# A two-layer conditioned linear attention kernel: transposes of the queries and of h by halves, a later film load, and a rearranged last unit

## The reference

```
xn = layernorm(x)
q = softmax over each head's channels (xn @ Wq + bq)
k = softmax over the tokens (xn @ Wk + bk, masked)
v = masked (xn @ Wv + bv)
att = per head: k^T v            (head size x head size)
y = per head: q att
scale, shift = split(silu(emb) @ W_emb + b_emb)      one row for each sequence
h = silu(layernorm(y) * (1 + scale) + shift)
x = x + h @ W_out + b_out
```

## Time and profile before

| | us |
|---|---|
| median of 3 runs | 811.47 (810.06 to 811.48) |
| the profiled execution | 811.12 |
| its span, first to last instruction | 809.2 |
| TensorE (PE) busy in it | 766.0 |
| VectorE (DVE) busy | 698.7 |
| ScalarE (ACT) busy | 517.0 |
| GpSimd (POOL) busy | 438.4 |

### The profile page before, as it was taken

How to read it: one execution, slowest core, us unless ns; L and a number is a source line. 1 busy time by engine, 2 the same in 40 slices (tenths; PEclk the granted TensorE clock), 3 DMA queues, 4 the chain that set the end, 5 groups by cost and what they waited for, 6 DMA issues and landing times.

```text
span 809.2 us, 16851 instructions
## 1 busy us (share of the span) xinstructions
PE 766.0 (95%) x6359; PEld 371.6 (46%) x6359; DVE 698.7 (86%) x1421; ACT 517.0 (64%) x1011; POOL 438.4 (54%) x432
## 2 busy tenths in 40 slices
PE   4997979999999999998999999999999999999986
PEld 2445434354444445444454544444454544444442
DVE  6898967798998999999988898888888899888985
ACT  4897763856748687686866685565657476560723
POOL 2475573553856658487563755447265535544352
PEclk9997989999999999999999999999999999999999
DMA  9966497664967759596594939588584939485542
GB/s 320 307 130 187 116 257 220 131 147 135 183 171 139 165 153 183 170 180 173 111 187 119 195 106 175 167 153 200 96 192 117 183 119 182 117 150 139 89 120 79
DMA packets 291201, 130.73 MB, mean 162 GB/s; under 512 B 261392, under 2 KB 261776, under 8 KB 291120
## 3 DMA queue, kind: packets, MB, share of 16 engines
q1 hardware_dynamic: 288384, 125.27, 68.7%
q10 hardware_dynamic: 2736, 4.39, 1.6%
HBM read 47.74 MB, written 16.88 MB: 80 GB/s over the span
## 4 chain that ended last, share of the span: by engine, by line
PE 80%; DVE 10%; issue 3%; ACT 3%; DMA 2%; POOL 1%; SPq 0%; DVEq 0%; ACTq 0%; POOLq 0%
PE ring L529 72%; PE ring L699 3%; PE att_ps L648 2%; DMA sb_ht_parts<-sb_htok 2%; DVE sb_k_or_qt L1021 1%; ACT sb_k_or_qt L1410 1%; DVE sb_q_sum L1080 1%; DVE sb_row_peak L868 1%; DMA sb_x<-in_x 1%; DVE sb_ht_parts L1134 1%; PE att_ps L590 0%; PE film_ps L590 0%; DVE sb_q_max L1054 0%; DVE ring L1051 0%; PE film_ps L599 0%
## 5 line engine op out<-in xcount | busy, mean ns | idle before, releaser
L529 PE MATMUL ring<-sb_w_hi,sb_xt_parts 128*128 128x512 f16 x1024 | 309.0, 379 | 0.0
L529 PE MATMUL ring<-sb_w_lo,sb_xt_parts 128*128 128x512 f16 x512 | 194.0, 379 | 0.0
L529 PE MATMUL ring<-sb_w_hi,sb_ht_parts 128*128 128x512 f16 x512 | 158.3, 384 | 10.0 <-DMA sb_ht_parts<-sb_htok 5.8
L529 PEld LDWEIGHTS ring<-sb_w_hi,sb_xt_parts 128*128 128x128 f16 x1024 | 100.3, 98 | 126.1 <-issue 6.6
L529 PE MATMUL ring<-sb_xt_parts,sb_w_hi 128*128 128x512 f16 x496 | 149.9, 384 | 8.6 <-issue 8.1
L1662 POOL TENSOR_TENSOR sb_htok<-sb_ht_parts,sb_htok 128x512 f16<-128x512 f32 x60 | 75.2, 1275 | 137.7 <-ACT sb_htok L1443 137.7
L1678 POOL TENSOR_TENSOR sb_tanh<-sb_v_or_q,sb_kq_hi 128x512 f16<-128x512 f32 x64 | 74.0, 1157 | 88.2 <-ACT sb_kq_hi L1474 87.6
L529 PE MATMUL ring<-sb_w_lo,sb_ht_parts 128*128 128x512 f16 x256 | 98.3, 384 | 0.0
L529 PE MATMUL ring<-sb_xt_parts,sb_w_lo 128*128 128x512 f16 x248 | 95.2, 384 | 0.0
L529 PEld LDWEIGHTS ring<-sb_w_hi,sb_ht_parts 128*128 128x128 f16 x512 | 50.7, 99 | 71.6 <-issue 9.7
L1467 ACT ACTIVATE sb_v_or_q<-ring,sb_ln_one 128x512 f32<-128x512 f32 x64 | 43.9, 686 | 61.6 <-DVE ring L1056 60.7
(11 more groups left out here) (230 smaller groups left out, 1403.1 us busy)
## 6 DMA issues: line engine op xcount, KB each, us to landing
out<-sb_x SPq DMA_DIRECT2D x14, 1024.0 KB, 4.8
sb_rows_now<-film_rows SPq DMA_DIRECT2D x16, 512.0 KB, 4.4
sb_x<-out SPq DMA_DIRECT2D x8, 1024.0 KB, 5.2
sb_x<-in_x SPq DMA_DIRECT2D x7, 1024.0 KB, 5.7
sb_mask_add<-mask_terms SPq DMA_DIRECT2D x15, 256.0 KB, 5.5
sb_w_stage<-in_L_cond_Wk SPq DMA_DIRECT2D x2, 1024.0 KB, 9.0
sb_w_hi<-in_L_cond_W_emb SPq DMA_DIRECT2D x1, 1536.0 KB, 13.1
sb_w_lo<-in_L_cond_W_emb SPq DMA_DIRECT2D x1, 1536.0 KB, 14.2
```

What stands on the lines that cost most here:

```text
L529: last = nc.tensor.matmul(out, lhs, rhs, start=(n == 0), stop=(n == len(pairs) - 1))
```

## The change

- `turn_q` and `turn_h` take a half j (0 or 1) and turn two token tiles, high and low. Each half has semaphores of its own. `ht_parts` is laid out by halves, so the first half of h overwrites y's tiles 0 and 1 only, and may be turned when these are split.
- TensorE waits for h by halves in `output` and for the queries by halves in `attend`.
- On SP, the film rows are loaded ahead of h (except in units 3 to 5), and the second half of x goes between the two halves of the queries.
- ScalarE asks for the second part of layer 1's film matrix behind the attention matrix of unit 1 instead of behind its values.
- Unit 14's output tiles use banks 0, 1, 0, 1. In unit 15, VectorE masks the attention matrix directly behind the queries' sums, and takes the reciprocals and residual 0 after it; GpSimd adds unit 15's output bias in unit 14; and `attended(LAST, 2)` comes ahead of the first low part of h.

```diff
-BANKS = {"K": (0, 1, 2, 3), ..., "Y": (2, 3, 4, 5), "last": (2, 3, 4, 5)}
+BANKS = {"K": (0, 1, 2, 3), ..., "Y": (2, 3, 4, 5), "next": (0, 1, 0, 1), "last": (2, 3, 4, 5)}
-    elif name == "O" and unit == LAST:
-        name = "last"
+    elif name == "O" and unit >= LAST - 1:
+        name = "last" if unit == LAST else "next"
...
-        ht_parts = sb("ht_parts", [P, 2, T, C, P], F16)
+        ht_parts = sb("ht_parts", [P, 2, 2, T // 2, C, P], F16)
...
-            def turn_h(u):
-                if u == 1:
+            def turn_h(u, j):
+                if j:
+                    pass
+                elif u == 1:
                     sp.wait_ge(v_lo_ready, 4)
                 else:
                     sp.wait_ge(done["O"], 4 * (u - 1))
-                sp.wait_ge(h_lo_ready, 4 * u)
-                turn(ht_hi.rearrange("p t c m -> p (t c) m"), flat_h[0], h_hi_ready, 4 * u, ht_hi_ready)
-                turn(ht_lo.rearrange("p t c m -> p (t c) m"), flat_h[1], h_lo_ready, 4 * u, ht_lo_ready)
+                h_count = 4 * (u - 1) + 2 * j + 2
+                sp.wait_ge(h_lo_ready, h_count)
+                for n, ready, turned in ((0, h_hi_ready, ht_hi_ready), (1, h_lo_ready, ht_lo_ready)):
+                    turn(ht_parts[:, j, n].rearrange("p t c m -> p (t c) m"), flat_h[n][:, 2 * j * D:2 * (j + 1) * D], ready, h_count, turned[j])
...
-            def turn_q(u):
-                sp.wait_ge(kt_hi_ready, 16 * (u + 1))
-                sp.wait_ge(kt_lo_ready, 16 * (u + 1))
-                turn(blocks_of(qt_hi), kq_hi[:], q_hi_ready, 4 * (u + 1), qt_hi_ready)
-                turn(blocks_of(qt_lo), q_lo, q_lo_ready, 4 * (u + 1), qt_lo_ready)
+            def turn_q(u, j):
+                if j == 0:
+                    sp.wait_ge(kt_hi_ready, 16 * (u + 1))
+                    sp.wait_ge(kt_lo_ready, 16 * (u + 1))
+                at = slice(2 * j * D, 2 * (j + 1) * D)
+                turn(blocks_of(qt_hi[:, at]), kq_hi[:, at], q_hi_ready, 4 * u + 2 * j + 2, qt_hi_ready[j])
+                turn(blocks_of(qt_lo[:, at]), q_lo[:, at], q_lo_ready, 4 * u + 2 * j + 2, qt_lo_ready[j])
...
                 turn_k(u)
-                turn_h(u)
+                if not PREP <= u < PREP + 3:
+                    sp.wait_ge(z_ready, 4 * u)
+                    load_rows(u)
+                turn_h(u, 0)
+                turn_h(u, 1)
...
-                sp.wait_ge(z_ready, 4 * u)
                 if PREP <= u < PREP + 3:
+                    sp.wait_ge(z_ready, 4 * u)
                     sp.wait_ge(shift_summed, 3 + u - PREP + 1)
-                load_rows(u)
+                    load_rows(u)
                 if u < LAST:
                     turn_x(u, 0)
-                turn_q(u)
+                turn_q(u, 0)
                 if u < LAST:
                     turn_x(u, 1)
+                turn_q(u, 1)
+                if u < LAST:
                     sp.wait_ge(x_new, 4 * u)
...
             def output(unit, tiles=range(T), between=lambda i: None):
-                project_tokens("O", unit, O_, ht_hi, ht_lo, tiles, between)
+                for t in tiles:
+                    if unit < LAST:
+                        pe.wait_ge(ht_hi_ready[t // 2], 16 * (unit + 1))
+                        pe.wait_ge(ht_lo_ready[t // 2], 16 * (unit + 1))
+                    project_tokens("O", unit, O_, ht_hi, ht_lo, (t,), between)
...
             def attend(u, between=lambda t: None):
-                pe.wait_ge(qt_hi_ready, 16 * (u + 1))
-                pe.wait_ge(qt_lo_ready, 16 * (u + 1))
...
                     if t % 2 == 0:
+                        pe.wait_ge(qt_hi_ready[t // 2], 16 * (u + 1))
+                        pe.wait_ge(qt_lo_ready[t // 2], 16 * (u + 1))
                         take_bank("Y", t, u)
...
                 query_sums(u)
+                mask_attention(u)
+                query_recip(u)
                 residual(u - 1, 0)
-                mask_attention(u)
                 residual(u - 1, 1)
...
-                last_h_low(0)
                 attended(LAST, 2)
+                last_h_low(0)
                 last_h_low(1)
...
                 high_values(u, range(T))
-                if u == 1:
-                    load_film_w(1, 1)
-                elif prepares is not None:
+                if prepares is not None:
                     copy_shift(1, prepares)
...
                 high_attention(u)
+                if u == 1:
+                    load_film_w(1, 1)
...
                 add_bias(u)
+                if u == LAST - 1:
+                    add_bias(LAST)
...
                 low_queries(u)
-                add_bias(u)
                 low_attention(u)
```

More of the change, by code:

```diff
@@ L70, in order @@
     return front + tiles_of("O", u - 1) + tiles_of("Y", u)
-BANKS = {"K": (0, 1, 2, 3), "first": (4, 5, 0, 1), "second": (2, 3, 4, 5), "O": (2, 3, 0, 1), "Y": (2, 3, 4, 5), "last": (2, 3, 4, 5)}
+BANKS = {"K": (0, 1, 2, 3), "first": (4, 5, 0, 1), "second": (2, 3, 4, 5), "O": (2, 3, 0, 1), "Y": (2, 3, 4, 5), "next": (0, 1, 0, 1), "last": (2, 3, 4, 5)}
 def bank_of(name, i, unit):
@@ L226, in build @@
         xt_hi, xt_lo = xt_parts[:, 0], xt_parts[:, 1]
-        ht_hi, ht_lo = ht_parts[:, 0], ht_parts[:, 1]
-        ht_f32 = ht_parts[:].rearrange("p n t c m -> p (n t c m)").bitcast(F32).rearrange("p (t d) -> p t d", t=T)
+        xt_tiles = [[xt_parts[:, n, t] for t in range(T)] for n in range(2)]
+        ht_hi, ht_lo = ([ht_parts[:, t // 2, n, t % 2] for t in range(T)] for n in range(2))
+        ht_f32 = ht_parts[:].rearrange("p j n t c m -> p (j n t c m)").bitcast(F32).rearrange("p (t d) -> p t d", t=T)
         tok_f32 = tok[:].rearrange("p n t d -> p (n t d)").bitcast(F32)
@@ L316, in build @@
         k_hi_ready, k_lo_ready, q_hi_ready, q_lo_ready = sem("k_hi_ready"), sem("k_lo_ready"), sem("q_hi_ready"), sem("q_lo_ready")
-        kt_hi_ready, kt_lo_ready, qt_hi_ready, qt_lo_ready = (
-            sem("kt_hi_ready"), sem("kt_lo_ready"), sem("qt_hi_ready"), sem("qt_lo_ready"))
+        kt_hi_ready, kt_lo_ready = sem("kt_hi_ready"), sem("kt_lo_ready")
+        qt_hi_ready, qt_lo_ready = ([sem(f"{name}{j}") for j in range(2)] for name in ("qt_hi_ready", "qt_lo_ready"))
+        ht_hi_ready, ht_lo_ready = ([sem(f"{name}{j}") for j in range(2)] for name in ("ht_hi_ready", "ht_lo_ready"))
         k_top_ready, k_shift_ready, k_exp, k_sum_scaled, k_recip_ready = (
@@ L767, in step @@
                     pe.wait_ge(w_ready[1], 2)
-                project_tokens("V", u, V_, xt_hi, xt_lo)
+                project_tokens("V", u, V_, *xt_tiles)
                 if u == B:
                     pe.wait_ge(w_ready[1], 3)
-                project_tokens("Q", u, Q_, xt_hi, xt_lo, between=with_q)
+                project_tokens("Q", u, Q_, *xt_tiles, between=with_q)
                 if shifted is not None:
@@ L1263, in tail @@
                 gate(LAST, 1)
+                attended(LAST, 2)
                 last_h_low(0)
-                attended(LAST, 2)
                 last_h_low(1)
@@ L1415, in high_keys @@
                 if u:
-                    act.wait_ge(qt_hi_ready, 16 * u)
+                    for j in range(2):
+                        act.wait_ge(qt_hi_ready[j], 16 * u)
                 for i in range(C):
@@ L1426, in tanh_of @@
                 elif unit == LAST:
-                    act.wait_ge(qt_lo_ready, 16 * UNITS)
+                    for j in range(2):
+                        act.wait_ge(qt_lo_ready[j], 16 * UNITS)
                 elif t == 0:
@@ L1439, in high_h @@
                 if t == 0 and unit:
-                    act.wait_ge(ht_hi_ready, 16 * unit)
+                    for j in range(2):
+                        act.wait_ge(ht_hi_ready[j], 16 * unit)
                 elif t == 0:
@@ L1656, in low_h @@
                 if unit:
-                    pool.wait_ge(ht_lo_ready, 16 * unit)
+                    for j in range(2):
+                        pool.wait_ge(ht_lo_ready[j], 16 * unit)
                 else:
```

27 lines of the change are left out of this document (14 added, 13 removed).

## The result

Before: 810.33 us, median of 20 runs (807.81 to 811.64). After: 815.33 us, median of 20 runs (811.20 to 819.75). The ratio is 1.0069 [1.0055, 1.0083]: the change made the kernel slower by 0.7%. Forecast were 798.0 and a range of 792 to 805. The runs after lie further apart than those before; the profiled execution, 813.17 with a span of 811.3, is one of the quicker ones, so it shows some 2 of the 5 us that the medians differ by.

The account below looks back on a forecast made before the run. TensorE, busy 95% of the span, was taken as the bound, so only its holes and halved clock could go. -9.5 - 2.0 - 1.5 = -13.0 us from 811.12 gave 798.1, stated as 798.0; range 792.0 to 805.0.

Parts of the forecast that it names:

- What bounds the kernel: TensorE, busy 95% of the span; 8.3 us of holes at unit starts await x's second half, last in SP's queue.
- Twelve halves at 1.4 are 16.8, so SP is through at 734.3: SP's queue, unit 14: started at 717.5, the last half lands at 736.2, before it is wanted at 737.95; holes close.
- the sum's largest term, -9.5: Unit starts: 8.3 us of holes and 1.7 of halved clock go, 0.5 given back for stray waits; bounds 0 to -10.0.
- rival (c): Middle of attend: last landing no earlier, +0.76 in ten units, 817.2 us, if a half costs over 1.55 us; chance 0.06.
- The load of the film rows moves into the pause of SP between the keys and h: SP's queue, each unit: 0.75 us of issue plus its transfer leaves the stretch between h and x, a gain.
- (a): Unit 1: the film matrix does no harm among the transposes, so the unit gives 7.7 us; 792.4 us, chance 0.14.
- (b): Only part of the holes closes: half of 9.5, nothing in unit 1, 1.0 at the end; 805.3 us, chance 0.14.
- (d): Nothing moves: holes lie inside TensorE's queue, not x's landing, and the tail's gain goes to the clock; 811 us, chance 0.04.
- Waits that are added: TensorE's waits per half of h in output and of q in attend; said of h's halves that they cost nothing.
- Unit 1: Wait for h goes, freeing 7.7 us, but the film matrix delays x's and q's transposes: -2.0 us, bounds +1 and -7.7.
- The last unit: Unit 15: earlier mask and freed banks start attend 2.2 us earlier, partly lost to clock: -1.5 us, bounds 0 and -2.3.

Follow-up runs that it names:

- a4_xfirst: Kernel before, whole transposes, with x's second half issued ahead of the queries: 814.92 us, ratio 1.0056.
- b2_xlast: a3_halves with both halves of the queries ahead of x's second half: 812.12 us, ratio 1.0020 to the kernel before.
- b3_rowsk: Kernel before with the film rows loaded ahead of the keys' transposes (except units 3 to 5): 810.00 us, ratio 0.9998.
- a3_halves: Changed kernel without its film-matrix and last-unit edits, so SP's order and the halves only: 818.70 us, ratio 1.0102 to the kernel before.
- b4_halves_rowsk: a3_halves with the film rows loaded ahead of the keys' transposes: 805.59 us, ratio 0.9943 to the kernel before.
- c1_after_rowsk: Changed kernel with only the film rows moved ahead of the keys' transposes: 802.10 us, ratio 0.9897 to the kernel before.
- d1_before_twice: Kernel before with a second, unread load of the film rows right behind the first in units 9 to 15: 813.46 us, ratio 1.0048.
- d2: Changed kernel with a second, unread load of the film rows right behind the first in units 9 to 15: 825.18 us, ratio 1.0212 to the kernel before.
- b1_rowsold: a3_halves with the film rows loaded behind h, as before the change: 813.04 us, ratio 1.0037 to the kernel before.
- a2_film: Kernel before with only the film matrix's load moved behind unit 1's attention matrix: 811.21 us, ratio 1.0016.
- c3_film2: Kernel before with the film matrix's second part asked for in unit 2, behind the first normalisation: 806.08 us, ratio 0.9948.
- a1_tail: Kernel before with the last unit's edits alone (banks, mask, bias, attended(LAST, 2)): 809.87 us, ratio 0.9994.
- d3_best_xlast: Changed kernel, rows ahead of the keys' transposes, film matrix asked for in unit 2, both query halves ahead of x's second: 794.33 us, ratio 0.9811.

## Why the prediction was wrong

**What bounds the kernel: right.** The transfer that is last in SP's queue sets where TensorE's holes stand (a4_xfirst, b2_xlast), and the kernels in which these holes are closed are the fast ones.

**"Twelve halves at 1.4 are 16.8, so SP is through at 734.3": the step that failed**, with the sum's largest term, -9.5. Over units 6 to 14 the twelve took 17.9 to 20.1 us, 1.50 to 1.68 a half. The 1.4 is a median, 1.29, with the 0.11 between two, and as a median it held: the median half took 1.27 in the changed kernel too. But a queue is as long as the sum of its halves, and each unit has some long ones. The kernel before showed them: the sixty halves of x behind that median go up to 4.30, and the mean of their sixty durations is 1.61. With the gap of 0.11 that is 1.72, above the 1.55 at which rival (c) took over.

The long halves come with the stops of the transfers. Unit 14, on which the sum was made, has none of over 0.9 us in this stretch in the kernel before. There a load of the kind "instruction" starts at 728.60, in SP's pause, and meets nothing. With the pauses gone such loads meet transposes nearly every time: 32 stops against 18. That this is why the halves got long is an argument from the traces; no experiment moved such a load.

The beginning was wrong as well. h's first half has its source early, but SP comes to it only when the keys' transposes and now the rows are issued. In unit 9 it started 18.84 us ahead of attend; forecast was 737.19 - 717.5 = 19.7. That is 0.85 late, and 19.88 - 16.8 = 3.1 came from the halves: 4.0 us in all. The forecast had the last landing 1.0 before attend's start; it came 3.0 behind it (513.27 - 510.27). The 1.9 us from SP's end to that landing were right (513.27 - 511.31 = 1.96). Whether a unit has a hole follows from the two numbers. The landing comes 1.96 behind SP's end and is wanted 0.9 behind attend's start, so a hole stands where the first number is less than about 1.1 above the second (us, from the changed kernel's profile):

| unit | h's start ahead of attend | twelve halves | hole in attend |
|---|---|---|---|
| 6 | 17.90 | 18.76 | 2.0 |
| 7 | 17.75 | 19.06 | 2.6 |
| 8 | 19.67 | 18.67 | 0.1 |
| 9 | 18.84 | 19.88 | 2.1 |
| 10 | 19.71 | 20.13 | 1.5 |
| 11 | 19.70 | 18.49 | none |
| 12 | 17.98 | 18.91 | 2.0 |
| 13 | 18.94 | 18.44 | 0.5 |
| 14 | 19.00 | 17.95 | none |

In unit 14, where the forecast was made, the hole did close, with nothing to spare:

```profile
722.86 0.77 SPq L398 DMA_DIRECT2D sb_rows_now<-film_rows  x1
723.82 6.29 SPq L408 DMA_TRANSPOSE sb_ht_parts<-sb_htok  x4
...
740.50 1.27 SPq L408 DMA_TRANSPOSE sb_k_or_qt<-sb_tanh  x1
```

**"The load of the film rows moves into the pause of SP between the keys and h"** took too much for free. That the move costs nothing with whole transposes (b3_rowsk moves them further, -0.2 us, interval -1.1 to +0.8) and that one place or the other is worth about 13 us with halves (a3_halves against b4_halves_rowsk, the changed kernel against c1_after_rowsk) is shown, and so is it by doubling the load (d1: 3.9, d2: 11.6). Why is only in part shown. It is not that the transfer engines are full from h to the last transpose in both kernels; that theory missed in a4_xfirst, b1_rowsold, b3_rowsk and d1_before_twice. In unit 14 before, with SP standing still from 727.45 to 729.38, the engines work on for 1.5 us and then have nothing to do for as long (same columns as above):

```profile
727.50:729.00 1.50, 1.50 (x8) 0.69 (x7) 1.50 (x6) 1.09 (x2) 0.82 (x1) 1.00 1.22 253
729.00:730.50 1.50, 1.50 (x8) 0.69 (x7) 1.50 (x3) 0.73 (x2) 1.21 (x2) 1.00 0.03 3
```

So the kernel before has slack there, which hides the rows, and the halves use it up. Nor are the engines what sets the pace of every half: behind a stop they moved 287 GB/s, in the steady queue 193, with SP's 1.25 us a half.

**Rival (c) happened**, which had 0.06. Its place was right: half of attend now stands behind the last landing as well as the next keys. Its point, 1.55 us for a half, was near: the nine units average 1.58. It does not tell one unit from another, though: unit 8 has 1.56 and no hole to speak of, unit 13 has 1.54 and one of 0.5, because h's start varies by 2 us (the table above). Its price was worked out as a shift of every unit (817.2), and the median came to 815.33. That the two come so close is partly luck: the holes of the profile, 11.5 us, are fewer and longer than it said, and the holes of unit 1 were no part of it. I knew the two numbers of this rival were 0.15 us apart, 1.55 and 1.4, and still gave it a chance as if 1.4 were the mean under the new load. The Trainium skill ("DMA: Bandwidth & Descriptors", Anatomy of one DMA) gives its fixed cost of about 2.0 us for GpSimd's path, and these transfers are SP's. The trace does not show it here: the four extra transfers per unit did not add 8 us but 0.5 (20.2 against 20.7 us in unit 9 for everything from h or the rows on).

**Rivals (a), (b) and (d) did not happen.** The film matrix did harm (a2_film), the kernel got slower and not faster, and the holes are landings (a4_xfirst).

**Waits that are added: "they cost nothing" held for h, not for the queries.** No wait in the middle of `output` shows. 11.5 us in seven pieces stand in the middle of attend.

**Unit 1: -2.0 forecast; unit 2's keys start 0.65 us later in the profile, and a2_film costs 1.3 us** (0.3 to 2.3, by its ratio). The reasoning held: the wait for h went, the matrix met x and the queries, and the lower clock followed. But the matrix was asked for at 109.47, not behind 112.2, so it met x's transposes as well as the queries', and the holes came to 8 or 9 us against some 4. Even without the matrix 5.0 us of holes stand there (c3_film2), which the forecast did not have. The profile's value is within the bounds given (+1 and -7.7), a2_film's just outside. The Trainium skill ("DMA: Bandwidth & Descriptors", Queues, rings and completion order) says that a DMA engine takes turns between the queues that have work for it; by that, transposes on SP's queue are slowed by a bulk load on ScalarE's and not only by what is ahead of them on their own. The trace agrees in so far as SP's issue of one half went from 1.26 to 5.41 us beside the matrix, with only the loads of the biases ahead of it that other units lack. It does not show the taking of turns itself.

**The last unit: -1.5 forecast, bounds 0 and -2.3.** In the two traces the end is 3.3 us (the changed kernel) and 2.3 us (a1_tail) shorter, with the mechanism as described. In the medians a1_tail shows 0.2, and at most 1.5. In c1_after_rowsk, beside b4, the tail's and the film's edits together are worth 3.7 us by the ratios, so where the rest of the kernel is even it does show. Part of the difference may be the hole of 0.95 that whole queries leave in a1_tail. Why its median shows so little is open.

**What stays open.** Loading the rows ahead of h instead of behind it (a3_halves against b1_rowsold, 0.65% or 5.3 us) is not seen in the profiled executions: from 240 to 765 us they have 8.9 us of these holes in a3_halves and 10.6 in b1_rowsold, and a3_halves's is its quickest execution. So the profiles of the changed kernel and of a3_halves explain the place of the loss and only a part of its size. The changed kernel's longest execution is also the one with the lowest mean clock (819.75 us at 0.980; the shortest 811.20 at 0.989), so holes near 2 us that do or don't bring the clock down may be a good part of it: after the hole of 2.13 in unit 9 the 48 products took 10.48 us, as at full clock, while in unit 12, behind one of 2.02, 144 took 32.78 where others take 31.19. This was not tried by itself. Why some transposes stop for 1 to 2.7 us, and whether the loads of kind "instruction" beside them do it, is open too.

```profile
514.15 10.48 PE ring L547 x48
...
652.50 32.78 PE ring L547 x144
```

## What to carry to other kernels

Price a queue of twelve transfers by their mean, not by the median: here 1.29 and 1.61 us were read from the same sixty rows, and the point at which the change turned from gain to loss lay between them. A pause in an issuing queue is also slack, into which late tiles, stops and extra loads fall unseen; before a wait is taken out, sum all transfers of the period, bulk loads on the same and on other queues included, and see whether the last landing moves. Here it did not move enough until one 512 KB load was sent off 7.6 us sooner. When the last transfer can't be made earlier, put last the one that is wanted last (b2_xlast is 6.6 us faster than a3_halves by the ratios, and d3_best_xlast the fastest of all).

## What the runs showed of the hardware

- SP's issue of a half took 1.23 to 1.31 us behind a pause and in a full queue alike. It was longer beside other traffic or a stop: 3.71 us as h's second half behind 512 KB of rows, 2.10 in a stretch in which the transfers moved 8 GB/s, and 5.41 beside a 2 MB load on another queue. A long issue row so marks a moment to look at.
- Transposes in flight stop now and then for about 1 to 2.7 us, 32 times in the changed kernel's trace, and at 30 of these a 16 KB load of kind "instruction" is under way. Such a load took 0.9 us and more without transposes beside it as well (0.96 at 515.68).
- The lower clock came behind holes of 2 us in one unit and not in another (unit 12 and unit 9 above). In unit 1 it began 0.5 us behind a hole of 4.15 us and lasted 10.3 us, through the second hole of 4.86 and into unit 2's keys.
- TensorE's busy time moves with its clock: 766.0 us at a mean of 0.985 (before, profiled), 761.0 at 0.992 (b3_rowsk, as fast in the median and with holes as long), 757.0 at 0.997 (d3_best_xlast), with the same 6359 products. So of these 9.0 us only 4.0 can go with the holes that were closed; the other 5.0 lie between two executions with the same holes.
